# Five chunk buffers and three remainder buffers in place of six and two

## What is computed

```python
x = x + relu(adj @ (item_feat @ W_item.T + b_item) + layernorm(x) @ W_user.T + b_user)
# then, on z = layernorm(x):
probs = softmax(z @ gate_w + gate_b); the two largest of 8 per row are kept, unnormalised
x = x + sum over the kept experts e of probs[e] * (gelu(z @ W1[e] + b1[e]) @ W2[e] + b2[e])
```

## Time and profile before

| | |
|---|---|
| median of 3 executions | 1466.82 us (1465.87 to 1469.14) |
| profiled execution, own time | 1460.35 us |
| its span, first to last instruction | 1458.5 us |
| granted TensorE clock | 0.998 |
| TensorE matmul busy | 1425.3 us (98%) |
| VectorE busy | 1256.8 us (86%) |
| ScalarE busy | 1094.7 us (75%) |
| GpSimd busy | 716.3 us (49%) |
| bytes moved by DMA | 489.44 MB, mean 336 GB/s |

### The profile page before, as it was taken

How to read it: one execution, slowest core, us unless ns; L and a number is a source line. 1 busy time by engine, 2 the same in 40 slices (tenths; PEclk the granted TensorE clock), 3 DMA queues, 4 the chain that set the end, 5 groups by cost and what they waited for, 6 DMA issues and landing times.

```text
span 1458.5 us, 20461 instructions
## 1 busy us (share of the span) xinstructions
PE 1425.3 (98%) x6682; PEld 1168.1 (80%) x6682; DVE 1256.8 (86%) x1775; ACT 1094.7 (75%) x1165; POOL 716.3 (49%) x397
## 2 busy tenths in 40 slices
PE   7999999999999999999999999999999999999898
PEld 6888888888888888888887778878888877777677
DVE  4889889889898898898898889889898989788787
ACT  4777767767777677677676878787888868787676
POOL 0004444533542443434335276877666784577830
PEclk9999999999999999999999999999999999999999
DMA  9999999999999999999999999989999998888860
GB/s 336 338 350 373 380 380 383 382 378 366 385 373 368 392 369 384 381 367 380 380 364 394 364 319 337 336 304 341 316 345 332 317 384 308 283 274 286 204 143 23
DMA packets 127335, 489.44 MB, mean 336 GB/s; under 512 B 26456, under 2 KB 32216, under 8 KB 126142
## 3 DMA queue, kind: packets, MB, share of 16 engines
q1 hardware_dynamic: 115422, 457.43, 85.0%
q0 software_dynamic: 11808, 30.71, 7.4%
HBM read 456.00 MB, written 40.99 MB: 341 GB/s over the span
## 4 chain that ended last, share of the span: by engine, by line
PE 78%; DVE 7%; issue 4%; POOL 4%; ACT 3%; DMA 2%; SPq 1%; DVEq 0%; ACTq 0%; POOLq 0%
PE p_agg L481 21%; PE p_agg L476 20%; PE p_agg L477 20%; POOL rr L1362 3%; DVE s_a_lo L936 3%; PE p_hid L569 2%; PE p_hid L571 2%; PE p_hid L570 2%; ACT s_a_hi L722 1%; PE p_agg L492 1%; PE p_hid L458 1%; PE p_small L522 1%; PE p_y L585 1%; PE p_y L587 1%; PE p_y L586 1%
## 5 line engine op out<-in xcount | busy, mean ns | idle before, releaser
L936 DVE TENSOR_TENSOR s_a_lo<-s_raw,s_a_hi 128x1500 fp32r<-128x1500 f32 x520 | 881.0, 1717 | 96.9 <-PE p_agg L481 55.8
L722 ACT ACTIVATE s_a_hi<-s_raw 128x1500 fp32r<-128x1500 f32 x520 | 749.8, 1454 | 187.0 <-PE p_agg L481 172.7
L476 PE MATMUL p_agg<-s_a_hi,s_h_hi 128*128 128x500 f32 x1560 | 624.8, 401 | 0.3 <-ACT s_a_hi L722 0.2
L477 PE MATMUL p_agg<-s_a_hi,s_h_lo 128*128 128x500 f32 x1560 | 605.8, 388 | 0.0
L481 PE MATMUL p_agg<-s_a_lo,s_h_hi 128*128 128x500 f32 x1560 | 443.1, 392 | 8.1 <-DVE s_a_lo L936 6.4
L1353 POOL DMA_INDIRECT zs<-s_rows,s_idx x136 | 235.2, 1729 | 257.6 <-DVE s_idx L1094 207.1
L1362 POOL DMA_INDIRECT rr<-s_ysb,s_dests x192 | 279.1, 1454 | 159.2 <-DVE s_ysb L1175 107.9
L481 PEld LDWEIGHTS p_agg<-s_a_lo,s_h_hi 128*128 128x128 f32 x1560 | 287.3, 188 | 86.7 <-DVE s_a_lo L936 28.3
L476 PEld LDWEIGHTS p_agg<-s_a_hi,s_h_hi 128*128 128x128 f32 x1560 | 293.9, 188 | 58.2 <-issue 3.5
L477 PEld LDWEIGHTS p_agg<-s_a_hi,s_h_lo 128*128 128x128 f32 x1560 | 294.1, 189 | 57.2 <-issue 3.4
L1329 POOL TENSOR_TENSOR s_gt<-s_ebase,s_gt 125x32 f32<-125x32 f32 x20 | 128.2, 6409 | 67.6 <-DVE s_gt L1020 67.5
(11 more groups left out here) (215 smaller groups left out, 1279.5 us busy)
## 6 DMA issues: line engine op xcount, KB each, us to landing
s_raw<-adj SPq DMA_DIRECT2D x520, 750.0 KB
s_wraw<-w SPq DMA_DIRECT2D x56, 256.0 KB
s_zt<-zs SPq DMA_DIRECT2D x48, 264.0 KB
out_s<-rr POOLq DMA_DIRECT2D x12, 512.0 KB
s_xtok<-x_tok SPq DMA_DIRECT2D x20, 256.0 KB
s_xt<-x_t SPq DMA_DIRECT2D x20, 250.0 KB
zs<-s_early SPq DMA_DIRECT2D x18, 264.0 KB
out_s<-s_x1s SPq DMA_DIRECT2D x17, 256.0 KB
```

Of the source, the lines that this page charges most:

```text
L476: mm(o, h_hi[:, k * D:(k + 1) * D], hi, start=(k == 0), stop=False)
L477: mm(o, h_lo[:, k * D:(k + 1) * D], hi, start=False, stop=False)
L722: fn(a_hi[:, n % HIS, :], raw[:, n % RAW, :], ACT.Copy).then_inc(hi_made, 1)
L936: tt(a_lo[:, n % LOS, :], raw[:, n % RAW, :], a_hi[:, n % HIS, :].bitcast(F32), ALU.subtract)\
```

## The change

The ring of loaded chunks gets one buffer less and the ring of remainders one more. The sum of the bytes is the same. No instruction is added, removed or moved on any engine; what changes is the buffer that each one names and the count that two waits (`load_raw`, `lo_chunk`) look for. The number of `raw_loaded` semaphores goes from six to five.

```diff
--- before.py
+++ after.py
@@ -21,7 +21,7 @@
 KC = 3
 CH = KT // KC
 NCH = BLOCKS * CH
-RAW, HIS, LOS = 6, 3, 2
+RAW, HIS, LOS = 5, 3, 3
 TAILP = 96
 EPS = 1e-5
 FEAT = 2
```

## The result

| | before | after |
|---|---|---|
| median of the executions | 1467.91 us (1465.87 to 1469.14, 4) | 1480.91 us (1476.52 to 1483.29, 4) |
| profiled execution, own time | 1460.35 us | 1482.42 us |
| its span | 1458.5 us | 1480.6 us |
| granted TensorE clock | 0.998 | 0.995 |
| TensorE matmul busy | 1425.3 us | 1431.8 us |

The changed kernel is slower by 0.99%: the ratio is 1.0099, with a 95% interval of 1.0078 to 1.012 (the ratio is the one on record; the two medians in the table are 0.89% apart). The forecast was 1467.8 us with a range of 1463 to 1475, so the result lies above the range. It lies where the slower rival stood, between its half (1475) and its whole (1483). The two profiled executions are 22 us apart where the medians are 13 apart: the one of before, 1460.35 us, is quicker than any other execution of that kernel on record.

The account below looks back on a forecast made before the run. TensorE was taken as the bound, with DMA close behind in the first stage. Terms -1.2 + 0 + 1.0 + 1.15 = +0.95 us, put on the 1466.8 us median, gave 1467.8 us, range 1463 to 1475.

Parts of the forecast that it names:

- the slower rival: Before 745 us and at both group starts, loads lose their cover: 1483 us whole, 1475 half; chance 0.23 in part or whole.
- The third remainder buffer: At c = 4 and 5 of 12 blocks before 745 us, earlier remainders remove 0.1 us of lateness each: 1.2 us gained.
- the 22 foretold: Sign in the first stage: late remainders at c = 13 and 17 stay, some 22 of 34 waits.
- The prediction's 0.56 us a load: For a plain chunk the remainder starts 0.56 us earlier, so its chunk load is issued only some 1.6 us later.
- The lost chunk buffer in the first stage: Before 745 us, loads issued some 1.6 us later mostly land where they land now, and the rest are covered: 0 us.
- The Trainium skill's rate: HBM to SBUF binds at about 358 GB/s per core, leaving no load slack; given no chance beyond the slower rival's.
- Where the experts begin: At 766 to 800 us, two delayed SyncE issues are mostly swallowed by the queue: 0.5 us each, 1.0 us lost.
- The second group: Weights issued at 1211.45 us and the tile behind them go out 1.15 us later; all of it shows: 1.15 us lost.
- Later tiles move by up to 2 us and keep their distance: Row tiles after the second group's start cost 0 us, with 2 us as the other end.
- The bubbles go: Faster rival: the 28.3 us of weight-load waits for `a_lo` vanish, 1453 us, or partly, 1462; chance 0.12 in part or whole.
- The third buffer stays empty: Rival: late roundings, with `HIS` = 3, hold remainders back; only the losses are left, 2.15 us, 1469; chance 0.10.

Follow-up runs that it names:

- 533: The changed kernel itself: five chunk buffers, three rounded-chunk buffers, three remainder buffers; 1480.91 us, ratio 1.0099 against the kernel before.
- 633: Against the kernel before: a third remainder buffer with six chunk buffers kept, room taken by shortening `h_lo`; 1462.91 us, ratio 0.9992.
- the three other traces: Five chunk buffers, expert transfers behind chunk loads: two remainder buffers (1.0137); the changed kernel with fill writes first (1.0066) or the block's own transfers first (1.0057).
- 532: Against the kernel before: five chunk buffers in place of six, remainder buffers left at two; 1485.09 us, ratio 1.0137.

## Why the prediction was wrong

**The third remainder buffer: right.** VectorE's wait for TensorE fell in the first stage from 51.2 to 1.0 us, and 32 late remainders are left there, more than the 22 foretold because loads now make some of them late; with six chunk buffers it is the 22. At c = 4 and 5 of block 8, the changed kernel's timeline (start, us) to set beside the earlier trace rows:

```profile
501.80 3.40 DVE L936 TENSOR_TENSOR s_a_lo<-s_raw,s_a_hi 128x1500 fp32r<-128x1500 f32 x2 [1.35 <-ACT s_a_hi L722]
...
505.78 0.85 PE L481 MATMUL p_agg<-s_a_lo,s_h_hi 128*128 128x500 f32 x3
...
507.82 0.85 PE L481 MATMUL p_agg<-s_a_lo,s_h_hi 128*128 128x500 f32 x3
...
509.86 0.84 PE L481 MATMUL p_agg<-s_a_lo,s_h_hi 128*128 128x500 f32 x3
```

The matmuls follow at 2.04 us both times; the 0.94 us group is gone. The term, 1.2 us, agrees with the 1 us of the run with six chunk buffers, within what can be told. At five chunk buffers the same buffer is worth some 5.6 us, a case the sum did not have. As I read it, not shown by a run: `lo_made` frees the chunk buffer, so a remainder held back by TensorE holds back the next load, and with no chunk lying ready every load counts. The means speak for little of this (a load is issued 10.80 us ahead of TensorE with two remainder buffers and 10.85 with three), so it would have to lie in the 53 waits of up to 2.4 us. The prediction's 0.56 us a load holds at six chunk buffers, where it is 0.5, and not at five.

**The lost chunk buffer in the first stage: the step that failed.** It said that "a load issued later finds the queue shorter", so that most loads land where they landed. They were issued 2.1 us later and landed 2.1 us later: the latency is 6.94 and 6.89 us, the time a chunk lay ready 1.97 and 0.37. The seventh buffer shows the same the other way, with loads issued 2.2 us earlier and a latency of 6.97. As I read it, not shown by a run of its own: at a DMA share of 0.99 the queue moved just what TensorE used, and a load issued later has the same bytes ahead of it, since those were issued later as well. I had read the 424 GB/s of the earlier trace rows as a reserve; it is a window of four us. At the same window the changed kernel shows 315 GB/s with a share of 0.96, so even four us vary by more than the margin I relied on. The rest of the step was nearly right: the time that chunks lay ready took 1.6 of the 2.1 us and the cover between rounding and matmul the other 0.5 (on average that cover is 2.63 us and not the 3.7 of the one chunk that I read). Of 719 us TensorE stood 3.0 us idle, and the stage lost 3.7 us where I had 0 and the rival 12. The same step set the terms of the two group starts, where the larger losses lie.

**The Trainium skill's rate.** Against the rule of the Trainium skill (DMA: Bandwidth & Descriptors, Where 436 GB/s comes from) I held the 375 GB/s of the earlier trace rows. The runs agree with me on the rate, 371 and 376 GB/s in this stage with 533 and 633. On the outcome the rule came nearer than I did: with five buffers few loads have slack. Loads landed one in 2.20 us on average, and the quickest quarter 1.83 us or less behind the one before, against the 2.02 us of a plain chunk on TensorE. The reserve was a tenth at best.

**Where the experts begin: 1.0 us foretold, 6.7 lost.** I priced two delays of SyncE one by one and let the queue swallow them. ScalarE and TensorE in the changed kernel:

```profile
786.48 1.46 ACT L722 ACTIVATE s_a_hi<-s_raw 128x1500 fp32r<-128x1500 f32 x1 [2.90 <-DMA s_raw<-adj]
...
793.98 1.45 ACT L722 ACTIVATE s_a_hi<-s_raw 128x1500 fp32r<-128x1500 f32 x1 [2.60 <-DMA s_raw<-adj]
...
795.49 0.50 PE L476 MATMUL p_agg<-s_a_hi,s_h_hi 128*128 128x500 f32 x1 [1.35 <-ACT s_a_hi L722]
...
798.71 0.49 PE L476 MATMUL p_agg<-s_a_hi,s_h_hi 128*128 128x500 f32 x1 [0.52 <-ACT s_a_hi L722]
```

ScalarE stands idle for loads before four roundings in a row, 2.90, 1.99, 2.60 and 1.77 us, and the cover of 3.7 us is used up. The rival names the group starts too, and this is its point ("landing slips by over about 2 us"). The fill writes and scattered rows need DMA time of their own there, as I read it; in this window (columns as in the earlier trace rows) TensorE is busy 2.65 of 4 us while DMA has no gap:

```profile
792.00:796.00 4.00, 2.65 (x11) 1.74 (x11) 1.67 (x2) 1.45 (x1) 0.00 (x0) 1.00 1.04 419
```

The order of the list gives back 2.3 of the 6.7 us; I put the rest down to the buffer itself, as a seventh gains 1.1 us there. How much of the rest is bytes and how much lateness carried in was not taken apart.

**The second group: 1.15 us foretold, 8.2 lost (3.7 to 4.3 in the three other traces).** I had the mechanism and mis-sized it twice. SyncE in the changed kernel, at the place of the earlier trace rows, and the remainder and the tile that belong to it:

```profile
1226.12 0.35 SPq L334 DMA_DIRECT2D s_wraw<-w  x1
...
1227.82 0.34 SPq L352 DMA_DIRECT2D s_zt<-zs  x1
...
1223.22 1.71 DVE L936 TENSOR_TENSOR s_a_lo<-s_raw,s_a_hi 128x1500 fp32r<-128x1500 f32 x1
...
1232.57 0.87 PE L560 MATMUL p_tp<-s_ident,s_zt 128*128 128x128 f32 x4 [2.10 <-DMA s_zt<-zs]
...
1271.70 0.66 PE L560 MATMUL p_tp<-s_ident,s_zt 128*128 128x128 f32 x4 [2.51 <-DMA s_zt<-zs]
...
1336.49 0.66 PE L560 MATMUL p_tp<-s_ident,s_zt 128*128 128x128 f32 x4 [0.71 <-DMA s_zt<-zs]
```

From the start of the remainder the weights go out after 1226.12 - 1223.22 = 2.90 us; before it was 1211.45 - 1210.47 = 0.98. That is 1.9 us later, not 1.15: the remainder ends at 1224.93, and from there to the weights it is 1.2 us where I had taken 0.4. TensorE's wait grew from 0.69 to 2.10 us, where I had named 1.8. Behind it came a cost that neither the prediction nor the rivals had, the granted clock. TensorE was busy 1.90 of the 4 us in which that wait lies, and in the next 4 us the clock was 0.59, at its lower level for most of the time; at the same place before, in 1218 to 1222 us, it was 1.00:

```profile
1229.00:1233.00 4.00, 1.90 (x10) 1.32 (x9) 2.90 (x4) 3.97 (x6) 0.00 (x0) 0.98 0.92 315
1233.00:1237.00 4.00, 4.00 (x15) 3.26 (x14) 3.90 (x7) 1.14 (x1) 1.69 (x1) 0.59 0.89 288
```

From this tile to the residual's matmul behind the next chunk (L501) it was 1221.01 - 1218.46 = 2.55 us before and is 1236.68 - 1232.57 = 4.11 us now, first before and then after:

```profile
1221.01 0.59 PE L501 MATMUL p_agg<-s_ident,s_xtok 125*128 125x125 f32 x4
```

```profile
1236.68 0.59 PE L501 MATMUL p_agg<-s_ident,s_xtok 125*128 125x125 f32 x4
```

So 1.6 of the 8.2 us are matmuls at the lower level. The three other traces with late tiles keep a clock of 1.00 there, which is part of why they lose less.

The second mistake is the larger: "Later tiles move by up to 2 us and keep their distance" is false. Tiles at 1271.70 and 1336.49 wait 2.51 and 0.71 us.

Why it reaches so many is seen in what SyncE waited for between 745 and 1370 us. Before:

```profile
SPq L294 <- DVE s_a_lo L936: 253.6, 119, 6.0
SPq L333 <- DVE s_wt L1149: 73.4, 40, 5.4
```

After:

```profile
SPq L294 <- DVE s_a_lo L936: 336.6, 123, 7.1
```

Before, 40 weight loads waited for their own buffer, at L333: SyncE was through with the chunk loads in time and each went as early as it could. Now that line is gone from the stage. Whenever SyncE comes to the weights it is already late, held by the chunk load in front. With the experts' issues first, the line is back:

```profile
SPq L333 <- DVE s_wt L1151: 84.9, 45, 5.4
```

and the tiles are in time. That late expert transfers cost the time behind chunk 478 is shown by these traces; how much of it a typical execution loses is not, since the ratio of that run, 1.0072, gives back some 4 us with an interval that reaches to nothing. The prediction had the 40 waits in its trace and did not read them.

**The rivals.** The slower one came true in its mechanism (the queue does not shorten, and landing slips past the cover). That its size came out too was luck, for its division was off: the blocks before 745 us lost 3.7 us and not 12, the group starts 14.9 and not 5. "The bubbles go" fell: 32 late remainders stayed. "The third buffer stays empty" fell by VectorE's 1.0 us and the 5.6 us between 532 and 533; but part of it is true: VectorE now waits 98.7 us for the rounding, and remainders came no earlier on average (2.00 and 2.02 us).

## What to carry to other kernels

How long loads wait in the queue said nothing here about how much prefetch could be given up; ask how long a landed tile lies before it is used, and take that as the reserve when DMA is busy near 0.99 of the time. With a ring one shorter, each issue moves by a whole step of the loop, and what it doesn't find in that reserve comes out of the cover of the engine behind. Read what the issuing engine waits for as well: a transfer that used to wait for its own buffer has no slack left once it stands behind a load that waits longer, and it is cheap to put it ahead. Where the ring has enough buffers, the order is worth nothing (1.0002 with six).

## What the runs showed of the hardware

In chunks 26 to 338 a load's latency did not depend on how far ahead it was issued as long as five buffers or more were in the ring: 6.97, 6.94 and 6.89 us on average with seven, six (the kernel before) and five (the changed kernel). It was 6.01 us with four and 5.16 with a quarter fewer bytes. A load of 112 KB at the start landed in 2.2 us, so a latency read in a busy stage is not that of a load by itself.

The quickest quarter of the loads landed 1.83 us or less behind the one before, which is 768,000 / 1.83 = 420 GB/s; the mean over the stage is 375 GB/s.

The granted clock fell to its lower level where TensorE had stood idle: to 0.59 in 1233 to 1237 us after an idle time of 2.10 us, and to 0.62 in 20 to 26 us after one of 5.74 us. A row of 500 columns is 0.62 us there and 0.39 us at the full clock. It did not fall after every such wait: it stayed at 1.00 after the 2.51 us before 1271.70 us. Where it fell, a late tile cost about twice what TensorE's wait for it had grown by (1.4 us of wait, 1.6 us of clock).

The value of a buffer is not a sum: a third remainder buffer gave about 1 us beside six chunk buffers and 5.6 us beside five; the list's order gave nothing beside six and about 8 us beside five (1.0099 and 1.0043).
